# A graph, attention and expert layer on one core: small loads moved behind x, first weights split during the norm, identity transposes while the matrix engine waits, edge slots in pieces of 28 and 137

## The chip, the cores and the metric

One core of a Trainium2 chip runs one program with hand-written queues and semaphores. The metric is the device time of one execution in microseconds. TensorE (PE) does the matmuls, VectorE (DVE), ScalarE (ACT) and GpSimd (POOL) the rest, and SyncE (SP) issues most of the transfers.

## The reference

Shapes: 625 tokens of 768 numbers, 20,625 edges, 12 heads, 16 experts with a hidden width of 1536.

```python
xn = _layernorm(x)
h = xn @ W                                   # graph convolution
norm = deg_inv_sqrt[src] * deg_inv_sqrt[dst]
gnn = segment_sum(h[src] * norm[:, None], dst) + b
q, k, v = xn @ W_qkv                         # attention with exponential features
q1, k1 = softmax_kernel_features(q), softmax_kernel_features(k)
mix = (q1 @ (k1.T @ v)) / (q1 @ sum(k1)) @ W_proj + b_proj
x = x + gnn + mix
x = x + experts(_layernorm(x))               # expert 0 for all tokens, 3 routed of 15
```

## The kernel before

Tokens lie in 5 tiles of 125 rows. A product in full precision is made as three products of rounded parts: each operand is split in a high part (ACT rounds it) and a low part (DVE subtracts the high part from the original). `split_high` (L497) and `split_low` (L502) do this for one half (384 columns) of a weight; the first half to be used is that of the graph weight, ("h", 0). They work in the order of `HALVES`, and semaphores `half_hi` and `half_lo` count them.

**The head of the kernel.** SP issues the edge indices (L575, L576), x in ten pieces (L579), then the weights for h, v and k (L580 to L585). ACT's own queue issues eight small loads at its very start: six pieces of the feature matrix into `prow` (L1353) and the two layer norm weights of the experts into `lnrow` (L1356). DVE turns edge indices into numbers (L869 to L874), marks for each edge which of 25 buckets (5 source tiles by 5 destination tiles) it belongs to (`ehot`, 25 instructions, L877), and then takes the statistics of x (L957), the inverse roots, and tiles 1 and 3 of the normalised rows `xn` (L984). ACT makes tiles 0, 2 and 4 of `xn` (L1366). PE transposes `xn` into eight PSUM tiles in the order of `T8`: six of four token tiles each, ("c", 0) to ("c", 5), and two that hold only token tile 4, ("l", 0) and ("l", 4) (L470). For each ACT copies the high part `xhi` (L1371, L1374) and DVE makes the low part `xlo` (L965, L968). These transposes share three PSUM banks in turn (`R3`), and so a transpose can wait until the low part of the tile three places earlier is made.

**Edges.** DVE makes a running count of the marks over all 25 buckets, a scan of 25 x 165 elements in two parts (`run`, L883), takes the totals per bucket (`bucket_totals`, L887), and the semaphore `etot_ok` tells PE. PE sums them over the partitions (`bucket_ranks`, L1639). With that DVE computes for each edge its place in a sorted table (`edge_slots`, L893, and `slots_of`, L905, which is called once for each entry of `HALVES_OF_EDGES`), and POOL stores the edges there, 165 indirect transfers in a row (L721). The table is read back when the adjacency counts are made, some 270 us later.

**What sets the order.** Each engine runs its own list strictly in order. On PE, `rows_times("h", {1: bucket_ranks})` computes h in ten groups of 18 matmuls (five token tiles by two halves), and calls `bucket_ranks` right after the second group:

```python
def bucket_ranks():
    pe.wait_ge(etot_ok, 1)
...
rows_times("h", {1: bucket_ranks})
rows_times("v")
```

On DVE the list before is: marks, statistics, xn, first scan (8 buckets), six low parts, low half of h 0, two low parts, second scan (17 buckets), totals, low half of h 1, slots of the first 82 edges of each partition, low half of v 0, slots of the other 83, and so on.

After this head come v, k, the key features, q, the product of keys and values (L1726), the attention, the output projection with the adjacency counts, the graph messages, routing and the loop over the blocks of the experts.

Of the kernel before, what the change touches and what calls it, by code (L numbers as in the profile page):

```python
# [23 lines left out]
ALU = mybir.AluOpType  # L24
ACT = mybir.ActivationFunctionType
# [4 lines left out]
C = D // 128  # L30
EDGES = 20625
ET = EDGES // TP
BUCKETS = NT * NT
# [2 lines left out]
BATCHES = (ET_TILES + BATCH - 1) // BATCH  # L36
EDGE_RANGE = 32768.0
IN_FLIGHT = 8
HALVES_OF_EDGES = [(0, ET // 2), (ET // 2, ET)]
OFFSETS = 16  # L40
REGION = [512 * (r // 4) + TP * (r % 4) for r in range(BUCKETS)]
COUNT_BANKS = (BUCKETS + 3) // 4
H, HD, M = 12, 64, 266
# [3 lines left out]
MC = 112  # L47
LR = 96
E, F = 16, 1536
FC = F // 128  # L50
# [57 lines left out]
def gps_kernel(nc, x, src, dst, gnn_w, gnn_b, w_qkv, w_proj, b_proj, proj_mat, gate_w, gate_b,  # L108
# [3 lines left out]
    with ctx:  # L112
# [44 lines left out]
        xn = at("xn", 162560, [TP, NT, D])  # L157
# [27 lines left out]
        ehot = at("ehot", 104192, [TP, BUCKETS, ET], BF16)  # L185
# [14 lines left out]
        ebucket = mid("ebucket", [TP, ET], F16)  # L200
# [52 lines left out]
        prow = at("prow", 177920, [MC, 3, 2 * HD])  # L253
        lnrow = at("lnrow", 177920 + 1536, [LR, 4, 128])
# [11 lines left out]
        ident = small("ident", [128, 128])  # L266
# [8 lines left out]
        projt = at("projt", s0, [128, M])  # L275
# [31 lines left out]
        bank = [banks[:, 512 * b:512 * b + 512] for b in range(8)]  # L307
# [11 lines left out]
        def groups(keys, banks):  # L319
            nonlocal turn  # L320
            for key in keys:
                b = banks[turn % len(banks)]
                turn += 1
                uses[b] += 1
                plan[key] = (b, uses[b])

        R3, R8 = [5, 6, 7], list(range(8))
        T8 = [("c", c) for c in range(C)] + [("l", 0), ("l", 4)]
        groups([("pt", 0)], R3)
        groups([("xt",) + k for k in T8], R3)  # L330
        groups([("lt", 0)], R3)
        groups([("h", i, s) for s in range(2) for i in range(NT)], R3)
        groups([("v", i, s) for s in range(2) for i in range(NT)], R3)
        groups([("k", o, s) for o in range(C) for s in range(2)], R3)
# [59 lines left out]
        def fill(pe, key):  # L394

            b, n = plan[key]
            if n > 1:
                pe.wait_ge(free[b], n - 1)
            return bank[b]

        def filled(last, key):
            last.then_inc(full[plan[key][0]], 1)

        def read(eng, key):

            b, n = plan[key]
            eng.wait_ge(full[b], n)
            return bank[b]

        def emptied(ins, key):  # L410
            ins.then_inc(free[plan[key][0]], 1)
# [48 lines left out]
        def turn_tokens(pe, name, rows, ready):  # L460

            for kind, k in T8:
                ps = fill(pe, (name, kind, k))
                if kind == "c":
                    todo = [(k, i, i) for i in range(4)]
                else:
                    todo = [(c, 4, c - k) for c in range(k, min(C, k + 4))]
                for c, i, place in todo:
                    ready(i)
                    last = pe.transpose(ps[:, place * TP:(place + 1) * TP], rows[:, i, 128 * c:128 * c + 128], ident[0:TP, 0:TP])  # L470
                filled(last, (name, kind, k))
# [25 lines left out]
        def split_high(act, name, s):  # L497

            act.wait_ge(ld_w[name], 16)
            act.activation(high_half(name, s)[:, :, :], wraw[name][:, :, 384 * s:384 * s + 384], ACT.Copy).then_inc(half_hi, 1)  # L500

        def split_low(dve, name, s):  # L502

            dve.wait_ge(half_hi, HALVES.index((name, s)) + 1)
            dve.tensor_tensor(wlow[name][:, :, 384 * s:384 * s + 384], wraw[name][:, :, 384 * s:384 * s + 384],
                              high_half(name, s)[:, :, :].bitcast(F32), ALU.subtract).then_inc(half_lo, 1)
# [67 lines left out]
        def _(sp):  # L574
# [6 lines left out]
            def load_qkv(name, a):  # L581
                sp.dma_start(wraw[name][:, :, :], w_qkv.rearrange("(c p) n -> p c n", c=C)[:, :, a:a + D]).then_inc(ld_w[name], 16)

            load_qkv("v", 2 * D)
            load_qkv("k", D)  # L585
            sp.wait_ge(epad_ok, 1)
# [262 lines left out]
        def _(dve):  # L849
            link = Chain(dve, dve_own)  # L850
            def norm(rows, to, p, own):
# [4 lines left out]
                for n in range(parts):  # L856
# [16 lines left out]
                                     op0=ALU.mult, op1=ALU.add)  # L873
            link(dve.scalar_tensor_tensor(out=ebucket[:, :], in0=eq[:, 0, :], scalar=float(NT), in1=eq[:, 1, :],  # L874
                                          op0=ALU.mult, op1=ALU.add))
            for b in range(BUCKETS):
                last = dve.tensor_scalar(ehot[:, b, :], ebucket[:, :], float(b), None, ALU.is_equal)  # L877
            link(last)

            def run(a, b):  # L880

                hot = ehot[:, a:b, :].rearrange("p b k -> p (b k)")
                return dve.tensor_tensor_scan(erun[:, a:b, :].rearrange("p b k -> p (b k)"),  # L883
                                              ones[0:TP, 0:1].broadcast_to([TP, (b - a) * ET]), hot,
                                              0.0 if a == 0 else erun[:, a - 1, ET - 1:ET], ALU.mult, ALU.add)
# [74 lines left out]
            def x_lower(kind, k):  # L960

                dve.wait_ge(xhi_ok, T8.index((kind, k)) + 1)
                ps = bank[plan[("xt", kind, k)][0]]
                if kind == "c":
                    ins = dve.tensor_tensor(xlo[:, k, 0:4 * TP], ps[:, 0:4 * TP], xhi[:, k, 0:4 * TP].bitcast(F32), ALU.subtract)  # L965
                else:
                    n = min(C, k + 4) - k
                    ins = dve.tensor_tensor(xlo[:, k:k + n, 4 * TP:N], ps[:, 0:n * TP].rearrange("p (c t) -> p c t", t=TP),  # L968
                                            xhi[:, k:k + n, 4 * TP:N].bitcast(F32), ALU.subtract)
                emptied(ins, ("xt", kind, k))  # L970
# [12 lines left out]
            for i in (1, 3):  # L983
                dve.tensor_scalar(xn[:, i, :], xs[:, i, :], lnrs[:, 3, i:i + 1], lnrs[:, 4, i:i + 1], ALU.mult, ALU.add).then_inc(xn_dve, 1)  # L984
            dve.wait_ge(const_ok, 1)
            link(run(0, 8))
            for kind, k in T8[:C]:
                x_lower(kind, k)
            split_low(dve, "h", 0)
            for kind, k in T8[C:]:  # L990
                x_lower(kind, k)
            link(run(8, BUCKETS))
            bucket_totals()
            split_low(dve, "h", 1)
            edge_slots()
            slots_of(*HALVES_OF_EDGES[0])
            split_low(dve, "v", 0)
# [349 lines left out]

        @block.scalar
        def _(act):
            for m in range(3):  # L1350
                rows = min(MC, M - MC * m)
                for half in range(2):
                    act.dma_start(prow[0:rows, m, HD * half:HD * half + HD],  # L1353
                                  proj_mat[MC * m:MC * m + rows, :]).then_inc(ld_proj, 16)
            for n, of in enumerate((ln_w, ln_b)):
                act.dma_start(lnrow[:, 2 * n:2 * n + 2, :],  # L1356
                              of.rearrange("(t e) (c p) -> (e c) t p", t=2, c=FC)).then_inc(ld_ln, 16)
            ps = read(act, ("pt", 0))
            emptied(act.activation(projt[:, :], ps[:, 0:M], ACT.Copy), ("pt", 0))

            act.wait_ge(const_ok, 1)
            act.activation(xhi[:, :, N], xpad[:, :], ACT.Copy)
            act.wait_ge(norm_ok, 1)
            for i in (0, 2, 4):
                act.wait_ge(ld_x[i], 32)
                act.activation(xn[:, i, :], xs[:, i, :], ACT.Identity, scale=lnrs[:, 3, i:i + 1],  # L1366
                               bias=lnrs[:, 4, i:i + 1]).then_inc(xn_ok, 1)
            for n, (kind, k) in enumerate(T8):
                ps = read(act, ("xt", kind, k))
                if kind == "c":  # L1370
                    act.activation(xhi[:, k, 0:4 * TP], ps[:, 0:4 * TP], ACT.Copy).then_inc(xhi_ok, 1)  # L1371
                else:
                    m = min(C, k + 4) - k
                    act.activation(xhi[:, k:k + m, 4 * TP:N], ps[:, 0:m * TP].rearrange("p (c t) -> p c t", t=TP),  # L1374
                                   ACT.Copy).then_inc(xhi_ok, 1)
                if n == 5:
                    split_high(act, "h", 0)
            ps = read(act, ("lt", 0))
            emptied(act.activation(lnwb[:, :, :, :].rearrange("p a e c -> p (a e c)"), ps[:, 0:4 * LR], ACT.Copy), ("lt", 0))
            split_high(act, "h", 1)  # L1380
            split_high(act, "v", 0)

# [225 lines left out]
        def _(pe):  # L1608
            pe.wait_ge(const_ok, 3)

            pe.wait_ge(ld_proj, 96)
            ps = fill(pe, ("pt", 0))
            for m in range(3):
                rows = min(MC, M - MC * m)
                last = pe.transpose(ps[:, MC * m:MC * m + rows], prow[0:rows, m, :], ident[0:rows, 0:rows])
            filled(last, ("pt", 0))
            turn_tokens(pe, "xt", xn, lambda i: pe.wait_ge(xn_dve, (i + 1) // 2) if i % 2 else pe.wait_ge(xn_ok, i // 2 + 1))
            pe.wait_ge(ld_ln, 32)
            ps = fill(pe, ("lt", 0))
            for m in range(4):  # L1620
                last = pe.transpose(ps[:, LR * m:LR * m + LR], lnrow[:, m, :], ident[0:LR, 0:LR])
            filled(last, ("lt", 0))
            for kind, k in T8[:C]:
                taken(pe, ("xt", kind, k))

# [400 lines left out]
```

## Time and profile before

| | us |
|---|---|
| median of 3 runs (lowest, highest) | 1203.5 (1202.85, 1204.97) |
| profiled execution | 1215.01 |
| its span | 1213.3 |
| PE busy in the span | 1144.9 (94%) |
| DVE, ACT, POOL busy | 761.9, 659.4, 469.2 |

The profiled execution is 11.5 us longer than the median; 1.7 us of it lie outside its span. Times in the rows count from the start of the span. The granted clock is a share of TensorE's full speed: 1.00 is 2.4 GHz and 0.50 is 1.2 GHz.

### The profile page before, as it was taken

The numbers are of one execution on the slowest core, as the hardware profiler recorded it, in microseconds if no ns is written. First come the engines' busy times: TensorE is split into PE (matmuls) and PEld (weight loads), VectorE is DVE, ScalarE is ACT, GpSimd is POOL, SyncE is SP. The second block draws the span as 40 slices with busy tenths as digits, with TensorE's granted clock in tenths as the row PEclk, the third lists the DMA queues.
The fourth block names the chain that finished last, engine by engine and source line by source line (L and its number), as shares of the span: only waits on it lengthen the run. The fifth ranks groups of instructions, "written<-read, shape, count | busy, mean of one in ns | idle before, by whom it ended". The sixth has DMA issues, their size and how long they took to land.

```text
span 1213.3 us, 20540 instructions
## 1 busy us (share of the span) xinstructions
PE 1144.9 (94%) x6373; PEld 1005.3 (83%) x6401; DVE 761.9 (63%) x1189; ACT 659.4 (54%) x1040; POOL 469.2 (39%) x340
## 2 busy tenths in 40 slices
PE   2999999999898999999999999999999999999995
PEld 2999998777665578888888999988888889999874
DVE  7951643266567647625676866656677786656983
ACT  4222574155500034337776874848767887486863
POOL 1188888787600100163213531212352354222521
PEclk9899999799999999999999999999999999999998
DMA  9030004140300222116876692746956969286943
GB/s 318 7 88 2 3 3 127 39 162 3 93 1 1 75 76 97 27 19 215 315 241 213 240 340 79 287 121 230 337 191 213 360 247 329 62 317 237 355 150 98
DMA packets 63088, 191.71 MB, mean 158 GB/s; under 512 B 14315, under 2 KB 15382, under 8 KB 63044
## 3 DMA queue, kind: packets, MB, share of 16 engines
q1 hardware_dynamic: 50276, 172.52, 38.8%
q0 software_dynamic: 11728, 18.27, 8.6%
q8 instruction: 27, 0.44, 0.2%
q10 hardware_dynamic: 1040, 0.33, 0.1%
q14 instruction: 17, 0.14, 0.0%
HBM read 178.74 MB, written 15.09 MB: 160 GB/s over the span
## 4 chain that ended last, share of the span: by engine, by line
PE 81%; DVE 7%; ACT 5%; issue 3%; DMA 2%; ACTq 1%; another core or an unknown queue 0%; DVEq 0%; POOL 0%; SPq 0%; POOLq 0%
PE banks L1927 25%; PE banks L1911 24%; PE banks L1659 5%; PE banks L1676 4%; PE banks L1691 3%; PE banks L1726 3%; PE banks L1895 3%; PE banks L1824 2%; PE banks L1849 2%; PE banks L1748 2%; PE banks L1899 2%; ACT kfeat L1421 2%; PE banks L1888 1%; PE banks L1737 1%; PE banks L1808 1%
## 5 line engine op out<-in xcount | busy, mean ns | idle before, releaser
L721 POOL DMA_INDIRECT edge_dram<-epair,eslot x165 | 214.5, 1300 | 100.1 <-issue 100.1
L785 POOL DMA_INDIRECT out<-ysb,sidx x27 | 117.0, 4332 | 239.9 <-issue 208.8
L519 ACT ACTIVATE w2hi<-w2raw 128x1536 fp32r<-128x1536 f32 x96 | 139.1, 1483 | 94.6 <-DMA w2raw<-in_L_ffn_fc_w 83.7
L532 DVE TENSOR_TENSOR w2lo<-w2raw,w2hi 128x1536 fp32r<-128x1536 f32 x96 | 164.5, 1753 | 26.9 <-ACT w2hi L519 23.8
L1927 PE MATMUL banks<-w2hi,hthi 128*128 128x384 f32 x624 | 161.7, 340 | 0.0
L1927 PE MATMUL banks<-w2hi,htlo 128*128 128x384 f32 x624 | 159.6, 336 | 0.0
L1927 PE MATMUL banks<-w2lo,hthi 128*128 128x384 f32 x624 | 159.1, 336 | 0.0
L519 ACT ACTIVATE w1hi<-w1raw 128x1536 fp32r<-128x1536 f32 x96 | 137.9, 1498 | 31.2 <-DMA w1raw<-in_L_ffn_fc_w 25.1
L1911 PE MATMUL banks<-w1hi,xthi 128*128 128x512 f32 x486 | 140.2, 397 | 2.2 <-POOL w1lo L532 2.2
L532 DVE TENSOR_TENSOR w1lo<-w1raw,w1hi 128x1536 fp32r<-128x1536 f32 x80 | 138.2, 1791 | 0.0
L1911 PE MATMUL banks<-w1lo,xthi 128*128 128x512 f32 x486 | 137.5, 391 | 0.0
L1911 PE MATMUL banks<-w1hi,xtlo 128*128 128x512 f32 x486 | 137.0, 391 | 0.0
L1514 ACT ACTIVATE hid<-banks,lnwb 128x128 f32<-128x128 f32 x324 | 116.0, 488 | 29.7 <-PE banks L1895 28.6
L857 DVE BATCH_NORM_STATS2 st<-hid 128x6 f32<-128x512 f32 x81 | 50.7, 682 | 118.3 <-ACT hid L1525 118.3
L1927 PEld LDWEIGHTS banks<-w2lo,hthi 128*128 128x128 f32 x624 | 113.3, 189 | 0.0
L1927 PEld LDWEIGHTS banks<-w2hi,htlo 128*128 128x128 f32 x624 | 113.2, 189 | 0.0
L1927 PEld LDWEIGHTS banks<-w2hi,hthi 128*128 128x128 f32 x624 | 112.0, 189 | 0.1
L1911 PEld LDWEIGHTS banks<-w1lo,xthi 128*128 128x128 f32 x486 | 91.7, 189 | 19.5
L1911 PEld LDWEIGHTS banks<-w1hi,xtlo 128*128 128x128 f32 x486 | 91.7, 189 | 19.4
L1911 PEld LDWEIGHTS banks<-w1hi,xthi 128*128 128x128 f32 x486 | 89.3, 189 | 19.2 <-issue 2.4
L1197 DVE TENSOR_TENSOR htlo<-hid,hthi 128x1536 fp32r<-128x1536 f32 x26 | 45.7, 1757 | 85.0 <-ACT hthi L1520 85.0
L532 POOL TENSOR_TENSOR w1lo<-w1raw,w1hi 128x1536 fp32r<-128x1536 f32 x16 | 60.8, 3802 | 31.9 <-remote 14.7
(344 smaller groups left out, 1852.5 us busy)
## 6 DMA issues: line engine op xcount, KB each, us to landing
w1raw<-in_L_ffn_fc_w SPq DMA_DIRECT2D x96, 768.0 KB
w2raw<-in_L_ffn_fc_w SPq DMA_DIRECT2D x96, 768.0 KB, 6.5
xs<-in_x SPq DMA_DIRECT2D x10, 336.0 KB
edge_dram<-epair,eslot POOLq DMA_INDIRECT x165
wg<-in_L_gnn_W SPq DMA_DIRECT2D x1, 2304.0 KB, 13.5
wv<-in_L_mix_W_qkv SPq DMA_DIRECT2D x1, 2304.0 KB, 19.9
wk<-in_L_mix_W_qkv SPq DMA_DIRECT2D x1, 2304.0 KB, 24.8
wq<-in_L_mix_W_qkv SPq DMA_DIRECT2D x1, 2304.0 KB, 10.2
```

The costliest lines, as they stand in the source:

```text
L519: act.activation(unit(w2hi if second else w1hi, second, u), unit(w2raw if second else w1raw, second, u), ACT.Copy).then_inc(w2_hi if secon ...
L532: eng.tensor_tensor(unit(w2lo if second else w1lo, second, u), unit(w2raw if second else w1raw, second, u), unit(w2hi if second else w1hi, ...
L721: pool.indirect_dma_start(out=edge_dram, out_offset=bass.IndirectOffsetOnAxis(ap=eslot[:, k:k + 1], axis=0), in_=epair[:, k, :].bitcast(I3 ...
L785: pool.indirect_dma_start(out=out, out_offset=bass.IndirectOffsetOnAxis(ap=sidx[:, 0:1], axis=0), in_=ysb[:, :], in_offset=None, bounds_ch ...
L857: last = dve.bn_stats(st6[0:p, n, :], rows[:, n * step:(n + 1) * step])
L1197: dve.tensor_tensor(lo[:, :, :].rearrange("p c t -> p (c t)"), hid[:, :], hi[:, :, :].rearrange("p c t -> p (c t)").bitcast(F32), ALU.subt ...
L1514: last = act.activation(hid[:, 128 * c:128 * c + 128], tr_ps[c // 4][:, 128 * (c % 4):128 * (c % 4) + 128], ACT.Identity, scale=lnw[:, bas ...
L1659: last = pe.matmul(ps[0:TP, 0:384], a[:, c, t], w, start=c == 0 and k == 0, stop=c == C - 1 and k == 2)
L1676: last = pe.matmul(ps[:, 0:b - a + b % 2], w, xt_[:, c, a:b + b % 2], start=c == 0 and k == 0, stop=c == C - 1 and k == 2)
L1691: filled(pe.matmul(ps[0:TP, 0:M], of[r:r + HD, h // 2, TP * i:TP * i + TP], projt[r:r + HD, :], start=True, stop=True), (name, i, h))
L1911: last = pe.matmul(hid_ps[n][:, :], a[:, c, :], w[:, c, 512 * n:512 * n + 512], start=c == 0 and k == 0, stop=False)
L1927: last = pe.matmul(y_ps[s][:, 0:384], a[:, c, :], w[:, c, 384 * s:384 * s + 384], start=c == 0 and k == 0, stop=False)
```

## The change

1. The eight small loads leave ACT's queue and go to SP's, behind x and the weight for h, ahead of the weights for v and k.
2. ACT's list: the high part of h 0 is made before `norm_ok` is waited for; tile 4 of `xn` is made after the fourth copy of the turned tiles and no longer before the first; the copy of the turned feature matrix (`projt`) comes after that of `lnrow`.
3. DVE's list: the low half of h 0 stands ahead of all eight low parts of x; the 25 bucket marks move from ahead of the norm to behind those low parts; the scan is cut at bucket 13 instead of 8, both parts stand behind the marks, and the low half of h 1 stands between them.
4. PE's list: 100 transposes of the identity into bank 0 stand first; the transposes of `prow` move behind those of `lnrow`.
5. Edge slots in pieces of 28 and 137 columns instead of 82 and 83.

`rows_times("h", {1: bucket_ranks})` is not touched.

```diff
+WARM = 100
+FIRST_EDGES = 28
+HALVES_OF_EDGES = [(0, FIRST_EDGES), (FIRST_EDGES, ET)]
...
@@ SP, behind the load of the weight for h
+            for m in range(3):
+                rows = min(MC, M - MC * m)
+                for half in range(2):
+                    sp.dma_start(prow[0:rows, m, HD * half:HD * half + HD],
+                                 proj_mat[MC * m:MC * m + rows, :]).then_inc(ld_proj, 16)
+            for n, of in enumerate((ln_w, ln_b)):
+                sp.dma_start(lnrow[:, 2 * n:2 * n + 2, :],
+                             of.rearrange("(t e) (c p) -> (e c) t p", t=2, c=FC)).then_inc(ld_ln, 16)
             load_qkv("v", 2 * D)
             load_qkv("k", D)
@@ DVE
             dve.wait_ge(const_ok, 1)
-            link(run(0, 8))
-            for kind, k in T8[:C]:
+            split_low(dve, "h", 0)
+            for kind, k in T8:
                 x_lower(kind, k)
-            split_low(dve, "h", 0)
-            for kind, k in T8[C:]:
-                x_lower(kind, k)
-            link(run(8, BUCKETS))
+            bucket_marks()
+            link(run(0, 13))
+            split_low(dve, "h", 1)
+            link(run(13, BUCKETS))
             bucket_totals()
-            split_low(dve, "h", 1)
             edge_slots()
             slots_of(*HALVES_OF_EDGES[0])
             split_low(dve, "v", 0)
@@ ACT
             act.wait_ge(const_ok, 1)
             act.activation(xhi[:, :, N], xpad[:, :], ACT.Copy)
+            split_high(act, "h", 0)
             act.wait_ge(norm_ok, 1)
-            for i in (0, 2, 4):
+            normal_rows(0)
+            normal_rows(2)
             for n, (kind, k) in enumerate(T8):
...
-                if n == 5:
-                    split_high(act, "h", 0)
+                if n == 3:
+                    normal_rows(4)
@@ PE
+            for n in range(WARM):
+                pe.transpose(bank[0][:, 0:128], ident[:, :], ident[:, :])
+            turn_tokens(pe, "xt", xn, lambda i: pe.wait_ge(xn_dve, (i + 1) // 2) if i % 2 else pe.wait_ge(xn_ok, i // 2 + 1))
```

## Rows read from the trace of the kernel before

**Rows 1.** The page, part 1: engine, busy us (share of the span), instructions

```profile
PE 1144.9 (94%) x6373; PEld 1005.3 (83%) x6401; DVE 761.9 (63%) x1189; ACT 659.4 (54%) x1040; POOL 469.2 (39%) x340
```

**Rows 2.** The chain that ended last, 0 to 130 us: start us, us, what

```profile
9.98 4.74 DVE lnst L957 x10
...
28.28 2.56 DVE wglo L505
30.84 0.60 DVE xlo L968
...
31.57 8.72 PE banks L1659 x36
...
40.30 0.03 PE banks L1644
40.33 56.86 PE banks L1659 x324
```

**Rows 3.** Instructions of DVE in order of time: start us, us, line, operation

```profile
7.04 2.91 DVE L877 TENSOR_SCALAR ehot<-ebucket 125x165 bf16<-125x165 f16 x25
...
31.67 6.06 DVE L883 TENSOR_TENSOR_SCAN erun<-ones,erun,ehot 125x2805 bf16<-125x2805 f32 x1
...
38.05 0.18 DVE L891 TENSOR_TENSOR etot<-elast 125x24 bf16<-125x24 f32 x1
38.14 2.55 DVE L505 TENSOR_TENSOR wglo<-wg,hi_h 128x2304 fp32r<-128x2304 f32 x1
...
41.94 5.47 DVE L908 SCALAR_TENSOR_TENSOR epos<-erun,efrom,ehot 125x82 f32<-125x82 bf16 x25
47.44 3.92 DVE L912 TENSOR_REDUCE evalue<-epos 125x82 f32<-125x2050 f32 x1
```

**Rows 4.** DMA, 0 to 34 us: a queue (packets, MB, share); an issue (KB, us to landing)

```profile
q10 hardware_dynamic: 1040, 0.33, 4.9%
...
wg<-in_L_gnn_W SPq DMA_DIRECT2D x1, 2304.0 KB, 13.5
```

**Rows 5.** Stretches: us, each engine's busy us, granted clock, DMA share, GB/s

```profile
4.00:12.00 8.00, 0.87 (x3) 0.47 (x3) 6.67 (x35) 1.78 (x3) 0.43 (x4) 1.00 1.05 260
14.00:18.00 4.00, 0.00 (x0) 0.00 (x0) 3.38 (x21) 0.01 (x1) 0.00 (x0) 1.00 1.03 401
200.00:207.00 7.00, 7.00 (x62) 6.58 (x62) 1.52 (x5) 0.85 (x2) 5.48 (x6) 1.00 0.99 257
```

**Rows 6.** Instructions of ACT in order of time: start us, us, line, operation

```profile
17.99 2.87 ACT L1366 ACTIVATE xn<-xs,lnrs 125x768 f32<-125x768 f32 x3 [6.46 <-DVE lnrs L980]
20.77 0.56 ACT L1371 ACTIVATE xhi<-banks 128x500 fp32r<-128x500 f32 x1
...
26.13 2.12 ACT L500 ACTIVATE hi_h<-wg 128x2304 fp32r<-128x2304 f32 x1
```

**Rows 7.** Transposes on PE in order of time: start us, us, line, operation

```profile
19.99 2.35 PE L470 MATMUL banks<-ident,xn 125*128 125x125 f32 x10 [0.24 <-ACT xn L1366]
...
27.09 0.52 PE L1621 MATMUL banks<-ident,lnrow 96*128 96x96 f32 x4 [0.49 <-DVE xlo L965]
```

**Rows 8.** Stretches with a low granted clock, columns as in rows 5

```profile
29.50:31.50 2.00, 0.00 (x0) 0.00 (x0) 2.00 (x3) 2.00 (x2) 0.00 (x0) 0.52 0.68 239
31.50:36.20 4.70, 4.63 (x15) 4.66 (x16) 4.70 (x2) 1.89 (x1) 0.00 (x0) 0.50 0.01 4
...
360.80:364.10 3.30, 3.30 (x12) 1.96 (x12) 0.34 (x1) 0.00 (x0) 0.00 (x0) 0.50 0.00 0
227.50:248.00 20.50, 18.66 (x81) 15.54 (x80) 8.23 (x25) 5.28 (x12) 16.52 (x14) 0.50 0.41 133
```

**Rows 9.** POOL, the first indirect transfer of an edge

```profile
54.67 2.68 POOL L721 DMA_INDIRECT edge_dram<-epair,eslot  x1 [50.11 <-issue]
```

**Rows 10.** The chain, 212 to 250 us, columns as in rows 2

```profile
217.59 4.41 PE banks L1726 x40
...
230.61 8.72 PE banks L1726 x40
```

More of the change, by code:

```diff
@@ L38 @@
 IN_FLIGHT = 8
-HALVES_OF_EDGES = [(0, ET // 2), (ET // 2, ET)]
+WARM = 100
+FIRST_EDGES = 28
+HALVES_OF_EDGES = [(0, FIRST_EDGES), (FIRST_EDGES, ET)]
 OFFSETS = 16
@@ L328, in gps_kernel @@
         T8 = [("c", c) for c in range(C)] + [("l", 0), ("l", 4)]
-        groups([("pt", 0)], R3)
         groups([("xt",) + k for k in T8], R3)
         groups([("lt", 0)], R3)
+        groups([("pt", 0)], R3)
         groups([("h", i, s) for s in range(2) for i in range(NT)], R3)
@@ L875, in _, with bucket_marks @@
                                           op0=ALU.mult, op1=ALU.add))
-            for b in range(BUCKETS):
-                last = dve.tensor_scalar(ehot[:, b, :], ebucket[:, :], float(b), None, ALU.is_equal)
-            link(last)
+            def bucket_marks():
+                for b in range(BUCKETS):
+                    last = dve.tensor_scalar(ehot[:, b, :], ebucket[:, :], float(b), None, ALU.is_equal)
+                link(last)
             def run(a, b):
@@ L1349, in _, with normal_rows @@
         def _(act):
[L1350 to L1359, printed above, removed]
             act.wait_ge(const_ok, 1)
             act.activation(xhi[:, :, N], xpad[:, :], ACT.Copy)
+            split_high(act, "h", 0)
             act.wait_ge(norm_ok, 1)
-            for i in (0, 2, 4):
+            def normal_rows(i):
                 act.wait_ge(ld_x[i], 32)
@@ L1375, in _ @@
                                    ACT.Copy).then_inc(xhi_ok, 1)
-                if n == 5:
-                    split_high(act, "h", 0)
+                if n == 3:
+                    normal_rows(4)
             ps = read(act, ("lt", 0))
             emptied(act.activation(lnwb[:, :, :, :].rearrange("p a e c -> p (a e c)"), ps[:, 0:4 * LR], ACT.Copy), ("lt", 0))
+            ps = read(act, ("pt", 0))
+            emptied(act.activation(projt[:, :], ps[:, 0:M], ACT.Copy), ("pt", 0))
             split_high(act, "h", 1)
@@ L1609, in _ @@
             pe.wait_ge(const_ok, 3)
+            for n in range(WARM):
+                pe.transpose(bank[0][:, 0:128], ident[:, :], ident[:, :])
+            turn_tokens(pe, "xt", xn, lambda i: pe.wait_ge(xn_dve, (i + 1) // 2) if i % 2 else pe.wait_ge(xn_ok, i // 2 + 1))
+            pe.wait_ge(ld_ln, 32)
+            ps = fill(pe, ("lt", 0))
+            for m in range(4):
+                last = pe.transpose(ps[:, LR * m:LR * m + LR], lnrow[:, m, :], ident[0:LR, 0:LR])
+            filled(last, ("lt", 0))
             pe.wait_ge(ld_proj, 96)
@@ L1616, in _ @@
             filled(last, ("pt", 0))
[L1617 to L1622, printed above, removed]
             for kind, k in T8[:C]:
```

## The prediction
> **What bounds the kernel now.** I read the page first: PE is busy for 94% of the span [rows 1], so time is to be had only where PE waits or runs at half clock. Then the chain of waits over the first 130 us, since the whole change lies there. It runs: statistics of x at 9.98, transposes of xn, high part of h 0, its low part until 30.84, two last low parts of x, and at 31.57 the first real matmul. From there PE is never idle on the chain for 65 us [rows 2]. So two moments matter: when h starts (31.57), and whether PE then has to stop. The place to look is the call of bucket_ranks after the second group of h: 36 matmuls from 31.57 end at about 40.3 [rows 2], and the totals that it waits for were written on DVE at 38.05 + 0.18 = 38.2 [rows 3]. The wait costs nothing before, with only 1.9 us to spare.
>
> **Loads.** The eight small loads on ACT's queue (q10) moved 0.33 MB and took 4.9% of 16 engines over 34 us, 1.7 us [rows 4]. Now they stand behind x and the weight for h, which landed at 5.76 (its issue) + 13.5 = 19.3 [rows 4]. I take all of the 1.7 us off: the weight lands at **17.6**. From both sides: nothing gained is 19.3; and if the small packets were also what holds x at 260 GB/s against 401 once only weights stream [rows 5], then 0.16 MB of indices, 1.92 MB of x and 2.36 MB of weight at 401 GB/s from about 2.5 give 13.6. Against the fast end speaks the second load of x, with no q10 beside it, which also ran at 257 GB/s [rows 5]; I stay near the slow end. At 257 GB/s, 2.09 MB of indices and x from about 2.7 us land by 10.9, and the statistics, freed of the 2.9 us of marks ahead of them, end at about 11.9 instead of 14.7. The norm, 3.3 us of small instructions, ends at 15.1 instead of 18.0. SP's list gets eight more issues between weights h and v; they are transfers needed after 27 us, and v and k have over 30 us of slack (used from 65 on, landed by 33).
>
> **ACT and the transposes.** ACT is in order, and the high part of h 0 now stands ahead of the rows of xn. So the norm's gain is not used: ACT waits for the weight until 17.6, rounds until 19.7 (2.1 us), and makes xn 0 and xn 2 until 21.6 (pitch 0.93) [rows 6]. Before, xn 2 was ready at 19.9 and the first copy of a turned tile began 0.84 later at 20.77 [rows 6]; now at 22.4. DVE idles from 16.4 to 19.7 and makes the low half of h 0 from 19.7 to 22.3, just in time. At the transposes' slow pace (208 ns each, 0.83 a tile of four) copies 0 to 3 start up to 24.9, xn 4 takes ACT until 26.5, the tile that needs it is turned at 27.6, and the last low part ends at **29.1**. At the fast pace the loop is limited by bank, ACT and DVE, and by the same steps I get 28.2. I take 28.8. So h can start at about 29, 2.7 us earlier than the 31.57 of before, and all that followed on the path before (rounding and subtracting h 0, 4.6 us) is out of the way. This is what the change gains.
>
> **The identity transposes.** Constants are there at about 4.3. A 128-wide transpose at the slow pace is 213 ns (10 xn transposes in 2.35 us, last one 0.41, is 0.216 [rows 7]). If the clock rises after some 4.8 us, the time it took the matmuls from 31.5 on [rows 8], the 100 end at about 17.7, before xn 2 is there: free. PE then waits for 3 to 4 us, so they do not carry a fast clock into h either; at best the xn transposes do. Do transposes raise the clock at all? Here they do: the four 96-wide ones at 27.09 follow each other at about (0.52 - 0.25) / 3 = 0.09 us, against 0.16 at the pace of 19.99, and nothing but transposes ran on PE in between [rows 7]. (The clock column of the profile says 1.00 already from the start; the spacing contradicts it before 26 us, and I go by the spacing.)
> The Trainium skill, TensorE: Matmul & The Clock Gate, Part 4: PE-mode transpose, says the contrary, that the full clock does not engage for transposes, since they do not count as busy in the same way. By that page the 100 would all run slow. The trace speaks against it.
>
> **The new wait.** This is where the sum turns. Between the last low part of x (28.8) and the totals, DVE now does, one after the other: 25 marks 2.94; scan of 13 buckets, 2145 elements at 6.06/2805 = 2.16 ns, 4.66; low half of h 1, 2.47 to the next start; scan of 12 buckets, 1980 elements, 4.30; totals 0.45 [rows 3]. With links that is 14.9 us, so the totals come at 28.8 + 14.9 = **43.7**. In the kernel before, 8 buckets and the marks were done while DVE would have idled, and low half h 1 came after the totals. PE starts h at 29, does its two groups in 6.3 (fast) to 8.7 us (slow) [rows 2] and stands at the wait from 35 to 38 on, for 6 to 8 us. Everything of PE queues behind it. It passes at 43.8, where before it passed at 40.2, a little ahead of the second of its two matmuls on the chain [rows 2]: **+3.6**.
>
> **The clock after it.** PE idles longer than before 29.5, when 1.9 us without work were followed by a granted clock of 0.50 [rows 8]. So groups 3 and on start at half clock. Price: 36 matmuls took 8.72, at 56.86/324 = 0.1755 each they take 6.32; 2.4 lost, part of it start-up, so **+2.3** [rows 2]. Bounds: 3.3 us of low clock as at 360.8, times the lost share (0.32 - 0.1755)/0.32 = 0.45, is 1.5; the whole low stretch of 29.5 to 36.4 under matmuls is 3.1 [rows 8]. The fast or slow clock of the first two groups does not matter, since PE waits after them anyway.
>
> **Edge slots.** The first piece of 28 costs DVE 25 x 0.16 + 1.4 + 2.0 = 7.5 us (the 82 wide one: 5.47 + 3.92 + 2.2 [rows 3]); it starts after the totals and edge_slots (1.7), at 45.4, and ends near 53. POOL starts at about 54 instead of 54.67 [rows 9], and so the 165 stores end about when they did. 28 entries last POOL 42 us at its 1.5 us pace; the 137 are done by 71. Low half v 0 is made by 55.5 and PE needs it near 71. Cost and gain nothing; DVE's later list (all 3 us later) stays ahead of a PE that is 6 us later.
>
> **Sum.** +3.6 + 2.3 = +5.9 in the profiled execution (1215.0 to 1220.9), and all behind this point waits on PE's own pace, so I put the same on the median: 1203.5 + 5.9 = **1209.4**.
>
> **Rivals.**
> (a) The 100 transposes stay slow. They end at 4.3 + 21.3 = 25.6; the first turned tile is copied at 26.7 instead of 22.4, the totals come 4.3 later: 1213.7. For it: only the rule above. Against: the lnrow spacing [rows 7]. 8%.
> (b) The streams were held back by the small packets alone: weight at 13.6, ACT ready for xn at 15.7 (norm 15.1 fits), totals at 39.8, PE passes 0.3 earlier than before, with the clock +2.0: 1205.5. Against: 257 GB/s of the second load of x [rows 5]. 8%.
> (c) Faster: the half clock of the key-value product. 40 such matmuls take 4.41 at full clock and 8.72 from 230.61 on [rows 10]; and the granted clock is 0.50 from 227.5 to 248, with PE busy for 18.66 us [rows 8]. By the same ratio that costs 18.66 x (1 - 4.41/8.72) = 9.2 us. If the shifted start let it stay at full clock, 5.9 - 9.2 = -3.3: 1200.2. It decides only if at least 8.3 us of that come back. Nothing in the change touches that stage. 4%.
> (d) Lateness is absorbed later by something tied to absolute time. I find only POOL's stores, which end at 319 whatever PE does, and nothing on the chain waits for them. Half of 5.9 back: 1206.5. 6%. The opposite, a further fall of the clock in such a stage, 1213: 4%.
> That the change is not slower through its own path needs the totals at 37.9 or earlier (40.2 - 2.3), so the weight at about 11.6; 4.44 MB cannot be there by then at 401 GB/s.
>
> **Numbers.** My forecast has 70%. About 0.2% (2.4 us) is what a measurement can tell from no change. Slower: 70 + 8 (a) + 4, most of (b) and of (d): 0.87. Faster: 0.05. Same: 0.08. The range holds the forecast with the weight's landing (17 to 19.3), the clock's 1.5 to 3.1 and reaches down to (b): 1205.4 to 1212.6.
>
> **What would show it.** Right: in PE's waits a wait of bucket_ranks' matmul for etot of 6 to 8 us, first matmul of h near 29, the 40.2 of before at 43.8; hi_h ahead of xn on ACT, starting at 17.6; granted clock 0.50 for 3 to 7 us from 43.8; L470 transposes from about 20. Wrong: totals before 40, hi_h starting before 15, identity transposes that end after 20, a clock of 1.00 through the stall, or a low stretch at 227 to 248 that is gone.

## The result and the profile after

| | before | after |
|---|---|---|
| median of 20 runs each (lowest, highest), us | 1203.97 (1202.41, 1206.53) | 1207.91 (1203.12, 1212.19) |
| ratio, 95% interval | | 1.0030 (1.0021 to 1.0040) |
| profiled execution, us | 1215.01 | 1207.74 |

The change makes the kernel slower by 3.9 us (the ratio gives 3.6). The two profiled executions stand the other way round, 1215.0 against 1207.7, so a difference of whole profiles says nothing here; stages have to be compared one by one. Even that has a limit: both profiles of the kernel before are of executions 11 and 12 us longer than this median (1215.0 and 1216.4), and no profile shows an execution of it near 1204.

First the head. The chain of the kernel after, 0 to 75 us (start us, us, what), which answers to [rows 2]:

```profile
5.74 12.57 DMA wg<-in_L_gnn_W
...
18.33 0.02 ACT hi_h L502
...
20.36 1.94 ACT xn L1370 x2
...
22.35 0.45 PE banks L472 x2
...
28.58 0.91 DVE xlo L981 x2
29.49 2.83 DVE ehot L890 x25
...
32.34 4.64 DVE erun L896
...
37.01 2.56 DVE wglo L507
39.57 4.27 DVE erun L896
...
44.38 0.28 PE banks L1654
```

The chain starts with the landing of the weight, goes to ACT (which rounds the weight before it makes xn), to the transposes and low parts, and then, where it used to pass to PE's matmuls, it stays on DVE: marks, scan, low half, scan, totals. From PE's side the same is one row of its waits (28 to 72 us), which says that PE waited once, for 6.5 us:

```profile
PE banks L1654 <- DVE etot L904: 6.5, 1, 6.5
```

And two stretches (columns as in rows 5). From 40 to 50 us PE is busy for 5.6 of the 10 us, and the granted clock is at its low level of 1.2 GHz (0.51); from 50.5 on it is back at the full 2.4 GHz.

```profile
40.00:50.00 10.00, 5.62 (x19) 5.62 (x20) 9.32 (x35) 0.00 (x0) 0.00 (x0) 0.51 0.00 0
50.50:52.00 1.50, 1.50 (x10) 1.50 (x9) 1.43 (x3) 0.49 (x1) 0.00 (x0) 0.99 0.00 0
```

The identity transposes, and the rows that answer to [rows 7]:

```profile
4.35 13.66 PE L1621 MATMUL banks<-ident 128*128 128x128 f32 x100 [4.35 <-POOL sel L718]
21.43 0.43 PE L472 MATMUL banks<-ident,xn 125*128 125x125 f32 x2 [3.41 <-ACT xn L1370]
```

The identity transposes ended at 18.0. At the slow pace 100 of them would have taken 21.3 us; they took 13.66.

Then the rest, by the starts of certain instructions. "Again" are second profiles of the same two kernels, taken with the experiments.

| start of, us | before | before again | after | after again |
|---|---|---|---|---|
| first matmul of h | 31.6 | 31.2 | 29.8 | 29.8 |
| bucket_ranks | 40.1 | 39.1 | 44.4 | 44.3 |
| first matmul of v | 65.5 | 64.4 | 72.6 | 71.8 |
| first matmul of k | 97.0 | 96.0 | 104.1 | 103.3 |
| first of the key-value product | 198.3 | 199.2 | 202.6 | 201.8 |
| its last | 238.9 | 233.9 | 236.6 | 235.8 |
| first of the output projection | 319.2 | 316.2 | 310.0 | 311.7 |
| last edge store (POOL) | 318.0 | 319.4 | 327.0 | 325.1 |
| first count matmul | 345.2 | 341.0 | 335.2 | 333.9 |

At v the change is 7.1 us behind (7.3 in the second profiles). Two more things are to be seen. The key-value product took 40.6 us in the first profile of before, where the granted clock was 0.50 for 20.5 us from 227.5 on [rows 8], the first 11 of them within the product, and 34.7, 34.0 and 34.0 us in the other three, at full clock. So the kernel before has it both ways. And in the two profiles of after the first count follows the last edge store by 8.2 and 8.8 us, where before it came 27 and 22 us later. The chain of after, 300 to 345 us, shows what that means in the first one:

```profile
325.46 1.19 POOL edge_dram L731
...
326.95 2.51 DMA edge_dram<-epair,eslot
...
329.74 2.33 DMA etab<-edge_dram
...
332.10 1.69 DVE ecode L1144
...
333.81 4.54 DVE oh L963 x4
```

POOL's 165 stores now stand on the chain, then the read back of the table, its conversion, the one-hots (the operands from which the counts are made). PE waited 2.90 us for them:

```profile
335.15 2.18 PE L1819 MATMUL banks<-oh 128*125 128x125 bf16 x16 [2.90 <-DVE oh L963]
```

In the second profile of after it did not wait there. The chain then runs through PE's own projection, and the first count comes 22.2 us after the first matmul of the projection, against 25.2 in the first profile:

```profile
311.72 19.60 PE banks L1835 x60
```

So in the changed kernel the two sides meet almost level: the table is the later one in one profile, PE in the other.

POOL started at 54.6 as before, yet ended 6 to 9 us later. POOL in order of time, after:

```profile
54.61 2.68 POOL L731 DMA_INDIRECT edge_dram<-epair,eslot  x1 [50.05 <-issue]
57.59 6.30 POOL L731 DMA_INDIRECT edge_dram<-epair,eslot  x1 [0.30 <-issue]
```

and DVE beside it:

```profile
56.76 6.07 DVE L921 SCALAR_TENSOR_TENSOR epos<-erun,efrom,ehot 125x137 f32<-125x137 bf16 x22
```

The second store took 6.30 us, and ended at 63.89, 1.06 after the last of DVE's 25 instructions of 137 columns (56.76 + 6.07 = 62.83). (The row has 22 of the 25; the window that it is from begins after the first three.) In the profile before, the second store took 1.32 us beside the 25 instructions of 83 columns. That one store is 5.0 us of the 9.0 by which the last store is later in the first profiles. The other 4 us are spread over the rest of the 165, and no run separates them.

### The profile page after: what moved, and what is told of

Its sections match the earlier page's. It is cut to its first block, busy times and chain, and to the rows that moved or that the text cites. A ratio compares the mean times of both kernels' runs of the same rounds, so it can differ in the third digit from the quotient of the medians.

```text
span 1205.9 us, 20740 instructions
## 1 busy us (share of the span) xinstructions
PE 1144.4 (95%) x6473; PEld 1011.2 (84%) x6501; DVE 761.3 (63%) x1189; ACT 656.9 (54%) x1040; POOL 468.7 (39%) x340
## 4 chain that ended last, share of the span: by engine, by line
PE 58%; POOL 19%; DVE 8%; issue 7%; DMA 4%; ACT 2%; ACTq 1%; DVEq 1%; SPq 0%; POOLq 0%
PE banks L1938 25%; PE banks L1922 22%; POOL edge_dram L731 18%; PE banks L1860 3%; PE banks L1906 3%; PE banks L1910 2%; DMA w2raw<-in_L_ffn_fc_w 1%; PE banks L1899 1%; DVE oh L963 1%; PE banks L1835 1%; DMA wg<-in_L_gnn_W 1%; DVE w2lo L534 1%; PE banks L1819 1%; DVE w1lo L534 1%; DVE erun L896 1%
## 5 line engine op out<-in xcount | busy, mean ns | idle before, releaser
L731 POOL DMA_INDIRECT edge_dram<-epair,eslot x165 | 223.5, 1355 | 100.0 <-issue 100.0
L795 POOL DMA_INDIRECT out<-ysb,sidx x27 | 103.6, 3836 | 257.9 <-issue 220.9
L534 DVE TENSOR_TENSOR w1lo<-w1raw,w1hi 128x1536 fp32r<-128x1536 f32 x80 | 141.2, 1827 | 0.0
L1523 ACT ACTIVATE hid<-banks,lnwb 128x128 f32<-128x128 f32 x324 | 116.0, 488 | 32.3 <-PE banks L1906 31.2
L534 POOL TENSOR_TENSOR w1lo<-w1raw,w1hi 128x1536 fp32r<-128x1536 f32 x16 | 58.8, 3673 | 31.6 <-remote 16.0
```

The lines of the kernel that those rows point to most:

```text
L534: eng.tensor_tensor(unit(w2lo if second else w1lo, second, u), unit(w2raw if second else w1raw, second, u), unit(w2hi if second else w1hi, ...
L731: pool.indirect_dma_start(out=edge_dram, out_offset=bass.IndirectOffsetOnAxis(ap=eslot[:, k:k + 1], axis=0), in_=epair[:, k, :].bitcast(I3 ...
L795: pool.indirect_dma_start(out=out, out_offset=bass.IndirectOffsetOnAxis(ap=sidx[:, 0:1], axis=0), in_=ysb[:, :], in_offset=None, bounds_ch ...
L1523: last = act.activation(hid[:, 128 * c:128 * c + 128], tr_ps[c // 4][:, 128 * (c % 4):128 * (c % 4) + 128], ACT.Identity, scale=lnw[:, bas ...
```

## The experiments

The experiments form three series, each on a chip of its own and with the kernel before measured beside it; ratios are to the kernel before in the same series. The first series is e1, e4, e5 and before_again, the second after_again, e6, e7 and e8, the third p1, p2, p3 and e10. In the first the kernel before itself had a median of 1219.1 us and lay anywhere from 1211.0 to 1226.4 in 29 executions, with low clock stretches of up to 24 us in the profiles. The ratios of that series are weak, and I read its runs by the starts of instructions in the head.

**e1, bucket_ranks later.**

```diff
-            rows_times("h", {1: bucket_ranks})
+            rows_times("h", {4: bucket_ranks})
```

> The changed kernel, with bucket_ranks called after the fifth group of h instead of the second. Theory (the new wait and the half clock after it cost the time): PE reaches the call at about 47, the totals are there at 44.4, so the 6.5 us wait and the half clock behind it go; the first matmul of v comes near 63 (65.5 in the kernel before, 72.6 in the changed one), and the median is 2 us below the kernel before, ratio 0.998, about 6 us below the changed kernel. Rival (the late edge table, which stands on the changed kernel's chain until 332, costs the time): little changes, ratio 1.002 to 1.004, since the stores start no earlier. Rival (luck of the clock in the key-value product): the first matmul of v moves as above, but the ratio stays anywhere from 0.995 to 1.005.

Measured: bucket_ranks at 45.3 without a wait, first matmul of v at **61.2** (72.6 after), but that of k at 97.5. Ratio 1.0017 (0.9992 to 1.0042), where 0.998 was expected. v comes 11.4 us earlier than in after; some of that is the clock of the first groups, high this time. So the wait and the clock behind it are the head's loss. But part of the gain was lost again within v: 36.3 us from v to k instead of 31.5, with PE waiting 3.0 us for the low half of v 1. In this execution the first count came 28 us after the last store, so the stores did not bind.

**e4, DVE's list of the kernel before.** Marks, scans and low halves in the old order, the rest changed.

```diff
-            def bucket_marks():
-
-                for b in range(BUCKETS):
...
+            for b in range(BUCKETS):
+                last = dve.tensor_scalar(ehot[:, b, :], ebucket[:, :], float(b), None, ALU.is_equal)
+            link(last)
...
+            link(run(0, 8))
+            for kind, k in T8[:C]:
+                x_lower(kind, k)
             split_low(dve, "h", 0)
-            for kind, k in T8:
+            for kind, k in T8[C:]:
                 x_lower(kind, k)
-            bucket_marks()
-            link(run(0, 13))
+            link(run(8, BUCKETS))
+            bucket_totals()
             split_low(dve, "h", 1)
-            link(run(13, BUCKETS))
-            bucket_totals()
```

> The changed kernel, with DVE's list of the kernel before (marks ahead of the norm, scan cut at 8, low half of h 0 after six low parts). Theory: the totals come at about 38.5, h starts near 32, no wait at bucket_ranks, so the time is that of the kernel before, ratio 1.000 (0.999 to 1.001). Rival (the loads and ACT's waiting for the weight cost the time): xn 2 is still at 22.3 instead of 19.9, and the ratio stays at 1.003.

Measured: h at 33.2, bucket_ranks at 41.0, v at 66.3 (65.5 before), k at 97.9; ratio 0.9991 (0.9966 to 1.0017). The theory's place and time hold. The head's loss is DVE's new order. The moved loads and ACT's new order gain nothing at v: h is 1.6 us later than before and v 0.8. The ratio agrees with the theory, and its interval is too wide to settle more. This kernel also had the long second store, 6.30 us at 54.5 beside 25 instructions of 137 columns, and here too the first count came 27 us after the last store.

**e5, pieces of 82 and 83.**

```diff
-FIRST_EDGES = 28
+FIRST_EDGES = 82
```

> The changed kernel with edge slots in pieces of 82 and 83 (here cut at column 82). POOL's first store moves from 54.6 to about 59. Theory (the table is only on the chain where the rest runs early): 0 to 2 us slower than the changed kernel, ratio 1.003 to 1.005. Rival (the stores set the time of the changed kernel): the whole 4 us are added, ratio 1.0065.

Measured: stores from 58.8 to 324.2, ratio 1.0039 (1.0009 to 1.0069), which does not tell the two apart. What it showed I had not asked for: the stores started 4.2 us later than after and ended 2.7 earlier. The first count came 30 us after the last of them, so this execution could not have shown stores that bind. Its second store took 1.33 us.

**before_again** (no edit).

> The kernel before, once more, for a second profile: the one shown ran 11 us above its median. Theory (the granted clock in the key-value product and the attention differs from one execution to the next): the low clock from 227.5 to 248 is shorter or gone, and the attention ends some 7 us or more earlier than at 312. Rival (it is in every execution and only profiling slows it): the same low stretch again.

Measured: 1216.4 us in a series where its median was 1219.1. The key-value product ran at full clock (34.7 us instead of 40.6); a low stretch of 6.8 us (236 to 243) came behind it. But the attention did not end 7 us earlier, only 3.3 (first matmul of the projection 316.2). The clock does differ from one execution to the next; it is not all that differs.

**after_again** (no edit).

> The changed kernel once more, for a second profile and a ratio beside the runs below. Theory: first matmul of v near 72.6 and that of k near 104, 7 us after those of the kernel before, in this execution too; ratio 1.003 to 1.006, the rest being what later stages give or take. The key features took 16.4 us in the first profile against 18.8 before: if that belongs to the change, it is 16.4 again; if it is chance, it is near 18.9.

Measured: 1204.7 against 1203.9, ratio **1.0013** (1.0004 to 1.0022), lower than the 1.0030 of the first comparison and than the 1.003 to 1.006 expected. v at 71.8, k at 103.3; key features 16.4 us again, while the four profiles of the first series and the first one of before have 18.8 to 19.6. Those five are executions of 1215 to 1224 us. All nine profiles with 16.4 are of 1193 to 1209 us, with bucket_ranks early or late. Kernels with the change stand on both sides, so it goes with the execution or the chip, though I did not find what it is. From the last key-value product to the first matmul of the projection it is the same: 80.3 to 85.7 us in the five, 73.4 to 77.4 in the nine.

**e6, e1 with v 1 ahead of the tile regions.**

```diff
+            split_low(dve, "v", 1)
             tile_regions()
             split_biases()
-            split_low(dve, "v", 1)
```

> The changed kernel with bucket_ranks after the fifth group of h, as in e1, and the low half of v 1 made ahead of the tile regions and the bias split. Theory (in e1 the gain at the first matmul of v, 61.2, was lost again because DVE's long second piece of slots made v 1 late): v 1 is ready near 75.5, before PE comes for it at 77, first matmul of k at 93 (97.5 in e1, 97.0 before), and the ratio is 0.997, 4 us below e1. Rival (something in the second half of v itself took the time): k stays near 97.5.

Measured: v at 63.3, k at **94.8**, projection at 303.3, 7 to 9 us ahead of after all the way, and yet ratio **1.0046** (1.0033 to 1.0059), where 0.997 was expected. The head went as expected and the time the other way. DVE could read the bucket sums only at 47.4, so the slots and the stores were 2.9 us late: last store at 330.7, first count at 338.8. PE arrived early and waited 13.3 us for the one-hots. This is what turned the question from PE to POOL.

**e7, the marks in DVE's idle time.**

```diff
+            bucket_marks()
             split_low(dve, "h", 0)
             for kind, k in T8:
                 x_lower(kind, k)
-            bucket_marks()
             link(run(0, 13))
```

> The changed kernel, with only the 25 bucket marks moved into DVE's idle time before the low half of h 0. Theory: totals 2.9 us earlier (41.4), the wait at bucket_ranks 3.6 instead of 6.5, first matmul of v near 69.7, about 3 us below the changed kernel, ratio 1.000 to 1.002. If the half clock after the wait goes too, 67.5. Rival (the wait is covered by something else): v stays at 72.6.

Measured: bucket_ranks 41.6, v 69.3, stores from 51.8 to 323.7, first count 331.9; 1202.8 us, ratio **0.9995** (0.9987 to 1.0004), 2.0 us less than after in the same series. Here bucket_ranks and the first store both came 2.8 us earlier, so e7 alone does not tell which counts. The expectation holds for v (69.7), and the ratio lies just under its range, within the interval.

**e8, all at once.** e7 and e6, rows 0 and 2 of xn ahead of the high part of h 0, and

```diff
-            rows_times("h", {1: bucket_ranks})
+            rows_times("h", {3: bucket_ranks})
...
-            split_high(act, "h", 0)
             act.wait_ge(norm_ok, 1)
...
             normal_rows(0)
             normal_rows(2)
+            split_high(act, "h", 0)
```

> All at once: marks in the idle time, rows 0 and 2 of xn ahead of the high part of h 0, bucket_ranks after the fourth group, v 1 ahead of the tile regions. Theory: h starts near 27.5, no wait at bucket_ranks, v near 60, k near 92, ratio 0.995 to 0.997 (5 us below the kernel before). Rival (the edge table, read back on the chain, takes the gain): k comes at 92 but the counts wait for the table, and the ratio is 0.999 to 1.000.

Measured: v 61.4, k 92.9, projection 299.8, but ratio **1.0043** (1.0029 to 1.0057). h came only at 29.6, not 27.5. The rival was right in its mechanism and even too mild: PE 10 us ahead of after, stores from 52.4 to 327.2, first count 335.4, again 8.2 after the last store, and again PE waited 13.3 us.

**p1, three pieces.** The test of the second store.

```diff
-HALVES_OF_EDGES = [(0, FIRST_EDGES), (FIRST_EDGES, ET)]
+HALVES_OF_EDGES = [(0, FIRST_EDGES), (FIRST_EDGES, 97), (97, ET)]
...
-            sp.wait_ge(eslot_ok, 2)
+            sp.wait_ge(eslot_ok, 3)
...
             slots_of(*HALVES_OF_EDGES[1])
+            slots_of(*HALVES_OF_EDGES[2])
```

> The changed kernel with edge slots in pieces of 28, 69 and 68 columns. Theory (POOL's second store takes 6.3 us because DVE's 25 instructions of 137 columns hold POOL off, which those of 83 columns did not; and where the rest runs without a low clock, the end of the stores sets when the counts begin, 8.2 us later): the second store is short again (1.2 to 1.4), the stores end near 320 instead of 325 to 327, and the ratio is 2 to 5 us lower than the changed kernel's 1.0013, 0.997 to 0.9995. Rival (a long store follows the first whatever DVE does): again 6.3, same time as the changed kernel.

Measured: 1200.6 us, ratio **0.9971** (0.9955 to 0.9987), against 1.0013 and 1.0030 for the changed kernel in other series. POOL in order of time, p1:

```profile
54.23 2.68 POOL L731 DMA_INDIRECT edge_dram<-epair,eslot  x1 [49.66 <-issue]
57.22 1.19 POOL L731 DMA_INDIRECT edge_dram<-epair,eslot  x1 [0.31 <-issue]
```

and DVE beside it:

```profile
55.57 5.13 DVE L921 SCALAR_TENSOR_TENSOR epos<-erun,efrom,ehot 125x69 f32<-125x69 bf16 x25
```

The second store is short again, 1.19 us, the last starts at 321.7 instead of 327.0 and 325.1, and the counts begin at 331.8 instead of 335.2 and 333.9, without a wait of PE and 10.1 us after the last store: PE sets them now. v is at 72.2 and k at 103.8, as in the changed kernel. The same wait of PE stands in the head, and the kernel is faster than before all the same.

**p2, e7 with three pieces.**

> e7 (marks in DVE's idle time) with the three pieces. Theory: stores end near 318.5 (323.7 in e7), matrix engine and stores about level at the counts, ratio 0.996 to 0.998 where e7 had 0.9995. Rival: PE sets the counts in e7 already, ratio 0.9995 again.

Measured: **1198.0** us, ratio **0.9952** (0.9935 to 0.9969). Stores 51.7 to 318.8, first count 328.9. PE does not wait at the counts here either. This is the fastest version, 6 us below the kernel before.

**p3, e8 with three pieces.**

> e8 (all at once) with the three pieces. Theory: the matrix engine reaches the projection near 300 as in e8, and the stores end near 322 instead of 327, so the counts begin near 330.5 and the ratio falls from 1.0043 to 1.000. That it is no faster than p2 although its head is 8 us shorter would show that the stores set the time. Rival (e8 was slow for its low clock from 324 to 345 alone): with or without the shorter stores the ratio stays at 1.004.

Measured: 1198.8 us, ratio 0.9960 (0.9946 to 0.9975); e8 had 1.0043. k at 93.5, over 7 us ahead of p2, but stores to 320.3 and first count 328.5, level with p2's 328.9, and no faster than p2. Here PE waited 2.90 us, and the stores set the counts. The rival (the low clock from 324 to 345 alone) fails as it was put. That stretch did go with the wait: 0.50 for 20.5 and 17.1 us where PE had waited 13.3 (e8, e6), for 6.8 to 6.9 us where it had waited 2.9 (after, e7, p3), and not at all from 329 to 345 where it had not waited (after_again, p1, p2). It cost little: from the first count to the first product of the experts' second layer after, e8 and p3 took 123.9, 125.2 and 123.8 us and after_again 123.8. The 6.9 us of the stores and this 1.4 are most of the 8.6 us between the medians of e8 and p3, which are of two series.

**e10, e6 without the identity transposes.**

```diff
-WARM = 100
+WARM = 0
```

> e6 without the 100 identity transposes. Theory: they only shape the clock of the transposes of xn and of the first groups of h; without them the xn transposes run at half clock, h starts at 30.0 to 30.8 instead of 30.0, and the first matmul of v comes at 63.3 to 64.5 (63.3 in e6). Rival (they carry the full clock into h): v 2 us later or more than in e6.

Measured, one execution of 1207.3 us: h at 29.9 (30.0 in e6), v at 63.2 (63.3), k at 94.7 (94.8). The transposes of xn ran slower (22 of them in 4.65 us from 22.22), DVE and ACT set the pace anyway. In the head the 100 transposes change nothing.

## Why the prediction was right, and where it was not

Forecast 1209.4 (1205.4 to 1212.6), slower; measured 1207.9. The direction and the place were right. The agreement in size is partly luck: the head lost more than forecast, less than that reached the median, and a second loss, at the stores, was not foreseen.

- **The weight's landing**, 17.6 forecast, 18.3 measured (5.74 + 12.57). The last piece of x was awaited until 12.2 instead of 10.9; it did not matter, since ACT waited for the weight. Rival (b), with the weight at 13.6, is out.
- **The last low part of x** 28.8 forecast, 29.49 measured. **DVE's list to the totals**, 14.9 forecast, 44.33 - 29.49 = 14.8 measured: prices taken from rows of the same instructions held within 0.1 us.
- **The new wait** at bucket_ranks, 6 to 8 us forecast, 6.5 measured; PE passed at 44.4 instead of 43.8, so +4.3 where I had +3.6. e1 and e4 show that this is the head's loss.
- **The clock after it.** From bucket_ranks to v 28.2 us instead of 25.4: +2.8, where I had +2.3. The granted clock was 0.50 from 40.3 to 50.5, the last 6.1 us of it under PE's work; 3 to 7 were forecast. Together 7.1 us in the head, forecast 5.9, and the mechanism (totals late, PE stopped, then low clock) as forecast.
- **The identity transposes** ended at 18.0 (17.7 forecast), and they raised the clock: 100 in 13.66 us, where the slow pace gives 21.3. Rival (a) is out, and with it, for this kernel, the statement of the Trainium skill (TensorE: Matmul & The Clock Gate, Part 4: PE-mode transpose) that transposes do not bring the full clock. They carried nothing into h, as forecast (e10).
- **The step that failed is "Edge slots ... Cost and gain nothing"**, and with it the sentence in (d) that nothing on the chain waits for the stores. Start (54.6) was right, the end was not: 327.0 instead of 318.0. I had read POOL's slack from a profiled execution that had spent some 9 us at low clock in the key-value product [rows 10] and was long in later stages too, and so reached the counts late. In the changed kernel the slack was gone: PE waited 2.90 us for the table in one profile and none in the other. One store took 6.3 us in place of 1.3. Taking it away lowered the ratio in each of three pairs, all between series: from 1.0013 to 0.9971 (p1), from 0.9995 to 0.9952 (p2) and from 1.0043 to 0.9960 (p3), the first with the head unchanged. How these 5 us come about in p1 is only in part shown. Up to the first product of the experts' second layer its profile gains 2.3 and 3.6 us on the two of after; the rest lies in the loop of the experts (see "Open"). The store is lost to the width of the second piece, which I had costed on DVE and not on the queue beside it.
- **The sum "all behind this point waits on PE's own pace"** is wrong for the same reason: the counts wait for the later of PE and the table. e6 and e8 show it sharply: PE 7 to 12 us ahead at the projection, and 0.43 to 0.46% slower than before. This doesn't explain why only 3.9 us (1.6 in the second comparison) of the head's 7.1 reached the median. How much of the 3.9 us is PE's and how much the stores' isn't settled either: no profile shows the kernel before in an execution near its median, so its own margin between PE and the table is not known.
- **Rival (c)** (the low clock of the key-value product) exists as a difference between executions: the product had the low clock for its last 11 us in the first profile of before, and not at all in the second or in both of after. The stretch of 20.5 us runs on into the attention, where the second profiles of both kernels have one of 6.8 us.

Open, first: what makes p1 and p2 faster than the kernel before. In p2 v comes 3.9 us later than in the first profile of before and the last store 0.8 us later, and yet the median is 6 us lower. In p1 they are 6.7 and 3.8 us later and the median 3.7 lower. Neither the head nor the stores can give that. Something else in the change, or in the usual executions of the kernel before, must be worth more than these differences, and no run looks for it.

Open, second: the profiled executions of p1 and p2 (1196.0 and 1193.2) are the lowest of their runs or within 0.02 us of it, and their expert loop took 725.5 and 725.6 us between the first and last product of the second layer, where the others took 729.1 to 733.6. A wait for the low part made on POOL, up to 4.4 us elsewhere, was absent in them, but it was absent in p3 too, whose loop took 729.7. Their medians carry the verdict, not these profiles; whether the shorter loop belongs to the three pieces or to chance isn't shown.

## What to carry to other kernels

When a step moves behind another on an in-order engine, follow its result to whoever waits for it: the moved marks and scans were cheap on DVE and cost PE a wait of 6.5 us and then its clock. Read the slack of a side queue from an execution in which the main engine was fast, or from the queue's own end: this one ended 27 us ahead of its reader in the profile before, and PE waited for it in the profile after. And after winning time ahead of a meeting point, look which side arrives last: in e8 PE was 10 us ahead, waited 13.3 us and was slower than before; with stores that ended 6.9 us earlier (p3) the kernel was 0.4% faster than before. Last, profile an execution near the median, or the stages of two profiles cannot be set against each other.

## What the runs showed of the hardware

**DVE holds off POOL's indirect stores, and how long depends on the width of its instructions.** With 25 instructions of 137 columns in a row, a store that began among them lasted 6.3 us in each of the kernels with that piece (after, e1, e4, e6, e7, e8, e10); in after it ended 1.06 us after the last of them. With 68, 69 or 83 columns the stores took 1.2 to 1.3 us. A single long subtraction with two inputs does the same. DVE and POOL in e8:

```profile
70.62 2.49 DVE L507 TENSOR_TENSOR wvlo<-wv,hi_a 128x2304 fp32r<-128x2304 f32 x1
```

```profile
70.98 3.19 POOL L731 DMA_INDIRECT edge_dram<-epair,eslot  x1 [0.30 <-issue]
```

The store ended at 74.17, 1.06 after the 73.11 of DVE. The Trainium skill, SBUF — State Buffer, on its two separate sides, tells of such a lock: a DVE operation in a two-port mode, or one with two inputs in SBUF against a POOL operation that reads SBUF, blocks POOL until it ends, and POOL cannot write the descriptors of a transfer that it issues. The single subtraction, with its two inputs, agrees. What that page does not tell is why a row of 25 short instructions holds POOL over all its gaps at 137 columns and not at 83; the runs show the difference and not its cause.

**The clock after a wait.** PE stood idle from 37.9 to 44.4, the granted clock was low from about 40 until past 50, and from bucket_ranks to v, 144 matmuls, it took 28.2 us instead of 25.4. The wait for the table did the same: 0.50 or 0.51 for 6.9 us after a wait of 2.90 us (after, p3), for 20.5 us around a wait of 13.32 (e8).
